# A graph layer on one core: the column sums of the first pass go through VectorE, and a product's first part moves ahead

## What is computed

```python
h   = relu(layernorm(x))                                   # 12500 x 128
m   = concat([h[src], 0, edge_attr]) @ W1 + b1             # 212500 x 256
m   = relu(batchnorm(m, g1, be1))                          # mean and variance over all edges
agg = segment_sum(m, dst) / maximum(count(dst), 1)         # 12500 x 256
n1  = relu(batchnorm(concat([h, 0, agg]) @ W2 + b2, g2, be2))   # 12500 x 385
out = x + relu(n1 @ W3 + b3)                               # 12500 x 128
```

## Time and profile before

| | |
|---|---|
| median of three runs | 3201.42 us |
| the profiled execution, its own time | 3181.97 us |
| its span, first to last instruction | 3180.2 us |
| granted clock of TensorE, mean | 0.856 |
| first pass, first to last gather | 145.9 to 2425.9 us |
| second pass and last stage | 2440 to 3180 us |

### The profile page before, as it was taken

How to read it: one execution, slowest core, us unless ns; L and a number is a source line. 1 busy time by engine, 2 the same in 40 slices (tenths; PEclk the granted TensorE clock), 3 DMA queues, 4 the chain that set the end, 5 groups by cost and what they waited for, 6 DMA issues and landing times. The chain is left out here.

```text
span 3180.2 us, 34295 instructions
## 1 busy us (share of the span) xinstructions
PE 2441.9 (77%) x12138; PEld 914.3 (29%) x12138; DVE 1393.9 (44%) x2299; ACT 969.7 (30%) x1601; POOL 1749.7 (55%) x1850
## 2 busy tenths in 40 slices
PE   4666767657767777777777677777867999999998
PEld 3412112112212222222222122222213433444448
DVE  4422212234323333322333233333223899999878
ACT  3322212112212221222122122212213655655546
POOL 6466666666666666666666666666664222222220
PEclk8888778778878888888888888888876999999999
DMA  8466656666656666666666566566664999999965
GB/s 237 155 210 215 212 194 224 209 221 239 216 194 227 212 213 207 218 204 207 216 229 208 190 223 218 195 228 220 212 206 150 337 350 350 345 343 345 341 238 162
DMA packets 270622, 740.85 MB, mean 233 GB/s; under 512 B 46391, under 2 KB 98661, under 8 KB 270448
## 3 DMA queue, kind: packets, MB, share of 16 engines
q1 hardware_dynamic: 189152, 525.28, 46.2%
q0 software_dynamic: 78432, 212.46, 22.4%
q10 hardware_dynamic: 2864, 0.86, 0.1%
HBM read 501.63 MB, written 236.81 MB: 232 GB/s over the span
## 5 line engine op out<-in xcount | busy, mean ns | idle before, releaser
L621 POOL DMA_INDIRECT sums<-P_d,late x1581 | 1496.5, 947 | 796.4 <-issue 453.3
L1052 DVE TENSOR_TENSOR sums<-psum,sums 128x1024 f32<-128x1024 f32 x396 | 479.0, 1220 | 1524.2 <-remote 823.9
L1351 PE MATMUL psum<-late,sums 128*128 128x512 f32 x1660 | 950.3, 687 | 255.2 <-issue 168.4
L709 ACT ACTIVATE sums<-sums 128x1024 f32<-128x1024 f32 x416 | 437.7, 1054 | 1720.7 <-remote 988.0
L1294 PE MATMUL psum<-sums,ones 128*32 128x512 f32 x830 | 486.5, 667 | 117.8 <-issue 70.2
L1351 PEld LDWEIGHTS psum<-late,sums 128*128 128x128 f32 x1660 | 315.4, 210 | 888.6 <-issue 728.0
L1297 PE MATMUL psum<-sums,ones 128*32 128x512 f32 x830 | 497.9, 676 | 59.5 <-issue 58.6
L1296 PE MATMUL psum<-sums,ones 128*32 128x512 f32 x830 | 494.5, 676 | 36.5 <-issue 35.9
L1295 PE MATMUL psum<-sums,ones 128*32 128x512 f32 x830 | 488.7, 670 | 28.8 <-issue 28.6
L1095 DVE TENSOR_TENSOR late<-late,psum 128x1024 f32<-128x1024 f32 (+1 forms) x407 | 482.6, 1212 | 34.3 <-DMA late<-m_d 32.5
L650 POOL TENSOR_TENSOR late<-dst_f,iota 128x384 f32<-128x384 f32 (+1 forms) x139 | 115.1, 829 | 379.4 <-PE psum L1463 375.3
(11 more groups left out here) (215 smaller groups left out, 2012.0 us busy)
## 6 DMA issues: line engine op xcount, KB each, us to landing
m_d<-sums SPq DMA_DIRECT2D x415, 512.0 KB
late<-m_d SPq DMA_DIRECT2D x406, 512.0 KB, 5.5
sums<-in_ea_main SPq DMA_DIRECT2D x103, 512.0 KB
sums<-P_d,late POOLq DMA_INDIRECT x1581
P_d<-sums SPq DMA_DIRECT2D x24, 512.0 KB
nodes<-in_x SPq DMA_DIRECT2D x24, 256.0 KB
late<-in_x SPq DMA_DIRECT2D x24, 256.0 KB, 3.1
out<-late SPq DMA_DIRECT2D x24, 256.0 KB, 2.4
```

Of the source, the lines that this page charges most:

```text
L621: pool.indirect_dma_start(out=m_s[s][0:r, k * L:(k + 1) * L], out_offset=None, in_=P1_d, in_offset=bass.IndirectOffsetOnAxis(ap=idx[0:r, G ...
L709: act.activation(q_s[g % Q_SLOTS][0:r, 0:w], m_s[g % M_SLOTS][0:r, 0:w], ACT.Square).then_inc(s_q, 1)
L1052: dve.tensor_tensor(m_s[s][0:r, 0:w], ps_m[place_m[g]][0:r, 0:w], m_s[s][0:r, 0:w], ALU.add).then_inc(s_m, 1)
L1351: ins = pe.matmul(ps_m[place_m[g]][:, 2 * i * L:2 * (i + 1) * L], ea[:, i * P:(i + 1) * P], W1c[:, :], start=True, stop=g not in xg_no, sk ...
```

## The change

- The statistics of a full group take two matmuls. ScalarE squares the second half of m into the group's own PSUM buffer, copies the second half of m beside it, and squares the first half into `q_s`. VectorE (`half_sums`) adds the halves of m into `half_s`, and the squares in place, and gives the new semaphore `s_sums`. It does this for group g-1 after the addition of g. PE multiplies `half_s` and `q_s` by the ones.
- What waited for `s_st` to reuse a slot of m (GpSimd's gathers, VectorE's additions in the twenty groups) waits for `s_sums`. ScalarE still waits for `s_st` of g-3, now for the slot that holds squares and half sums.
- A PSUM buffer is free with `s_sums` of its group, no longer with `s_m`.
- `odd_rows(b, 0)` of all 25 blocks moves from the second pass into every second counting step of the first. Its accumulator is now in bank 5 beside the counts, cleared by VectorE at the beginning, and `ps_n` and `empty_bank` use banks 4 and 6 in its place. The weights for k = 0 are ready from the beginning (`s_oddw` counts to 2).
- `totals`, `pick` and the copies at the end of the pass have 64 partitions in place of 128.

```diff
-                act.activation(q_s[g % Q_SLOTS][0:r, 0:w], m_s[g % M_SLOTS][0:r, 0:w], ACT.Square).then_inc(s_q, 1)
+                m, q = m_s[g % M_SLOTS], q_s[g % Q_SLOTS]
+                if g < GF:
+                    act.activation(ps_m[place_m[g]][:, 0:2 * L], m[:, 2 * L:], ACT.Square)
+                    act.activation(ps_m[place_m[g]][:, 2 * L:], m[:, 2 * L:], ACT.Copy)
+                    act.activation(q, m[:, 0:2 * L], ACT.Square).then_inc(s_q, 1)
+                else:
+                    act.activation(q[0:r, 0:L], m[0:r, 0:L], ACT.Square).then_inc(s_q, 1)
...
+            def half_sums(g):
+                m, q, other = m_s[g % M_SLOTS], q_s[g % Q_SLOTS], ps_m[place_m[g]]
+                dve.wait_ge(s_q, g + 1)
+                dve.tensor_tensor(half_s[g % Q_SLOTS], m[:, 0:2 * L], other[:, 2 * L:], ALU.add)
+                dve.tensor_tensor(q, q, other[:, 0:2 * L], ALU.add).then_inc(s_sums, 1)
...
                 if g in ranges:
                     ranges[g]()
+                if g >= 1:
+                    half_sums(g - 1)
...
                 if g >= M_SLOTS:
                     pool.wait_ge(s_mw[s], 16 * (g // M_SLOTS))
-                    pool.wait_ge(s_st, g - M_SLOTS + 1)
+                    pool.wait_ge(s_sums, g - M_SLOTS + 1)
...
-                pe.wait_ge(s_q, g + 1)
-                last = GF - 1
                 if g < GF:
-                    pe.matmul(ps_tot[0:32, :], ones[:, 0:32], m[:, 0:2 * L], ...)
-                    pe.matmul(ps_tot[32:64, :], ones[:, 0:32], m[:, 2 * L:], ...)
-                    pe.matmul(ps_tot[64:96, :], ones[:, 0:32], q[:, 0:2 * L], ...)
-                    ins = pe.matmul(ps_tot[96:128, :], ones[:, 0:32], q[:, 2 * L:], ...)
+                    first, last = g == 0, g == GF - 1
+                    pe.wait_ge(s_sums, g + 1)
+                    pe.matmul(ps_tot[0:SPAN, :], ones[:, 0:SPAN], half_s[g % Q_SLOTS], ...)
+                    ins = pe.matmul(ps_tot[SPAN:2 * SPAN, :], ones[:, 0:SPAN], q, ...)
...
+                if q in own_at:
+                    ins = odd_rows(own_at[q], 0)
                 ins.then_inc(s_cnt, 1)
...
-                    pe.wait_ge(s_xTs if gathered else s_m, i + 1)
+                    pe.wait_ge(s_xTs if gathered else s_sums, i + 1)
...
-                    for b in first_odd_at.get(g, []):
-                        odd_rows(b, 0)
```

More of the change, by code:

```diff
@@ L106, in build @@
     init_at = {early_at[b] if b < EARLY else SG * due[b - 2] + 6: b for b in range(NB)}
-    first_odd = [g for g in range(4, FIRST) if g not in init_at]
-    first_odd_at = {g: [b for b in range(NB) if b * len(first_odd) // NB == i] for i, g in enumerate(first_odd)}
     halves_at = {SG * due[b] - 2 + 3 * h: (b, h) for b in range(NB) for h in range(halves(b))}
@@ L704, in _ @@
             for g in range(NG):
-                r, w = rows(g), tiles(g) * L
+                r = rows(g)
                 act.wait_ge(s_m, g + 1)
@@ L1301, in stats, with odd_rows @@
                 ins.then_inc(s_st, 1)
+            def odd_rows(b, k, start=False):
+                pe.wait_ge(s_oddw, 2 if k else 1)
+                if k:
+                    pe.wait_ge(s_b2, 1)
+                    pe.wait_ge(s_n0, b + 1)
+                v = (nodes, plane[0], plane[1])[k]
+                for t, a, r in tiles_of(b):
+                    ins = pe.matmul(ps_odd[t * SPAN:(t + 1) * SPAN, 0:r], odd_col[:, k, SPAN - 1 - b:2 * SPAN - 1 - b],
+                                    v[:, a:a + r], start=start, stop=(b == NB - 1 and k == KC - 1),
+                                    skip_group_check=True)
+                if k == KC - 1:
+                    ins.then_inc(s_oddacc, 1)
+                return ins
```

62 lines of the change are left out of this document (28 added, 34 removed).

## The result

The changed kernel took 3351.8 us (median of 4 runs, 3342.8 to 3383.6) beside 3202.4 us for the kernel before (3198.4 to 3209.1) on the same chip: a ratio of 1.048, 95% interval 1.041 to 1.056. It is 150 us slower. The forecast was 3149 us, faster; 3352 also lies above the range of 2930 to 3310.

A forecast was written before the change was run, and what follows sets the result against it. GpSimd's gather issue rate was taken as the first pass's floor, with some 330 us of waits on top. Waits -47, own part -7 and pass end +2 made -52 us, from 3201 to 3149 us, range 2930 to 3310.

The forecast's parts named there:

- part 6: PSUM buffers held until s_sums: two-group loop about 4.7 us warm, 6.6 at lower clock, under 2 x 5.0; no steady cost.
- part 4: Slot release for GpSimd's gathers moves two to three groups forward in PE's order: some 10 to 15 us of slack.
- The sum: First-pass wait cycle lengthens from 30.2 to 48 us; 47 waits of 5.2 us, 247 us in place of 294.
- the slow stretches: First-pass times when PE starts few matmuls (11 in 16 us), recurring every 30.2 us with GpSimd waits of mean 3.9 us.
- Part 1: Statistics on PE, four matmuls to two: worth 0 in fast stretches; one and a half times as far in slow ones.
- Parts 2 and 3: ScalarE's three operations take 1.7 us, +0.65 a group; VectorE's two half sums add 1.35 us; both hidden as throughput.
- Part 5: Slot release through VectorE's waiting addition and two half sums: each wait left grows by up to 2.6 us, to 6.5.
- Part 7: Own part of the one-column product leaves the start of the second pass: gain 7 us, bounds 0 and 8.
- Part 8: End of the first pass: last full group goes through three ScalarE operations and half sums, +2 us on the path.
- Rival D: Longer release decides: 75 to 88 waits in the first pass each 1.35 to 2.6 us longer, 3315 us; chance 0.30.
- Rival B: Added slack covers slow stretches that end by themselves, taking nearly all long waits away: about 2900 us; chance 0.18.
- Rival C: Waits come back at the same total at the new gate, net -5 us: 3196 us; chance 0.10.

The follow-up runs named there:

- sbuf_sums: Changed kernel with half sums made from SBUF, one whole-slot ScalarE square, and the PSUM buffer free with the addition again: 3259.0 us, 1.021 of the kernel before.
- hold_only: Kernel before with PE's edge matmuls of group g waiting for VectorE's addition of g-2 in place of g-3, nothing added: 3198.8 us, ratio 1.0035.
- lateness made by hand: Edge matmuls' report given one group later for some 260 of 416 groups: kernel before 3197.4 us, changed kernel 3634.3, half sums from SBUF 3295.6.
- own_only: Kernel before with only the nodes' own part of the one-column product moved behind the counts, no half sums: 3190.6 us, ratio 1.0002.
- the first set: Follow-up runs on one chip with late PE reports, changing buffer hold, half sums, own part or gathers: kernel before 3190.1 us.
- the last set: Kernel before, changed kernel and half sums from SBUF, each with reports delayed, on a chip with late reports: kernel before without the delay 3189.6 us.
- the three between: Second, third and fourth sets of follow-up runs, on chips without late reports: kernel before 2845.3, 2843.9 and 2848.2 us.

## Why the prediction was wrong, point by point

**The failed step is part 6**, the PSUM buffer held until the half sums: "so it costs nothing in a steady state, and eats about 5 us of the slack of part 4". On that the sum took 75 long waits to 47 of 5.2 us. The traces count 74 before and 81 after, 4.0 and 6.0 us each: they didn't get rarer, and each got longer. With the hold undone (sbuf_sums) there are 42, near the 47. So, as far as sbuf_sums tells, the hold ate not 5 us of the slack but all of it.

What part 6 left out of its loop is the time between the end of the edge matmuls and VectorE's knowing of it. As an estimate from the rows: over two groups the loop is 4.7 us + lateness against 2 x 5.0 us, which bears some 5 us of lateness, and here one report in ten is at least 11 to 13 us late. The kernel before frees the buffer with the addition alone, over three groups: 1.92 + 1.22 us + lateness against 15 us, which bears some 12 us. This sum isn't the whole account: by it hold_only (3.1 us + lateness against 10 us) bears some 7 us, less than the latest tenth, and yet it lost only 9 us.

**What is shown and what isn't.** That the loss needs the chips with late reports is shown: 1.048 there, 1.0003 for the same kernel without them. That it goes through the buffer's release by the half sums is shown from two sides: without that release some 80 of 149 us come back, and lateness made by hand adds some 295 us with it, 37 and 8 us without. The 69 us that stay in sbuf_sums stand beside slower gathers (+104 us), which the changed kernel doesn't have; that it would be ahead of the kernel before without them is a sum and not a run, since slower gathers also leave fewer waits. Not shown is how the addition, the two half sums behind it and the rest share the cost: hold_only, the addition alone, cost 9 us, and the runs with ScalarE's square or the column sums in the loop fell on chips without lateness. For the square the trace of the changed kernel speaks: half sums waited 6.3 us in all for it. Open, too, is why PE's reports and its own instructions come late there.

**What bounds the kernel**: the rows were read rightly as to who waits, and only in part as to why. "PE's releases come in bursts" was seen, and the slow stretches were treated as PE running slow, to be shortened by fewer instructions. PE did start instructions late, but the waits end on its reports, and these came late even for matmuls that were long done.

**Part 1**, column sums worth 0 in a fast stretch: right, 0.59 to 0.62 us each pair as before. The bonus for a slow stretch, "one and a half times as far", +8 us of the cycle, has nothing behind it: the long waits came as often as before.

**Parts 2 and 3**: right in size, 1.80 us of ScalarE (0.60 + 0.58 + 0.61, I took 1.7) and 1.36 us of VectorE (1.35).

**Part 4**, slack of two to three groups: sbuf_sums, which has this release and not the hold, has 42 long waits in place of 74, though its slower gathers had a part in that. **Part 5**, each wait longer by up to 2.6 us: by 1.9 us. The sum took half of the 2.6, 1.3.

**Part 7**, own part: I took 7 us. From the first group of the second pass to the end some 5 us went (718.3 and, in own_only, 718.8 us, before 723.6), and own_only as a whole measured 0 (-5 to +6). **Part 8**, +2 us at the end of the pass: 33.3 us in place of 30.7 from the last gather on, one trace each.

**Rival D**, 3315 us with 0.30, is what came, and in its own terms: as many waits as before, each longer by 1.35 to 2.6 us (measured 1.9), and its two signs, waits ended by a half sum and "edge matmuls that wait for s_sums rather than for nothing", are the first rows above. It came out 37 us short; it was priced at its near end, 1.35 us a wait. That reports are late, and that nothing of this happens on other chips, was in no rival. **Rival B** spoke of slow stretches that end by themselves. In the kernel before, 168 of the 209 reports that are over 5 us late come while GpSimd pauses, up to 5.4 us after its last gather ended, and 41 while gathers go on. That fits what the prediction held against B, but as GpSimd waits for these reports, which of the two ends the other isn't shown. **Rival C** is what chips without late reports show, for another reason: in the kernels with these gathers traced there GpSimd has one wait of over 2 us in all.

## What to carry to other kernels

Where a buffer's release passes through an engine's report, put the lateness of the report into the loop beside the operations, and read it from the trace: end of the instruction that raises the semaphore against the start of the one that waited for it. A wait with the releaser "remote" that ends long after the work was done can be such a lateness and not a gap in the record. Count the long waits and their length apart: here their number stayed and their length grew. Measure a change of this kind on more than one chip. Don't let the release of a PSUM buffer go through further work behind its reader in a kernel whose matmul reports are late, even if all the work in the loop is hidden. One group less of room by itself cost 9 us here.

## What the runs showed of the hardware

PE's semaphore increments can be recorded up to 27 us after the matmul that gives them while GpSimd issues indirect gathers all the time (1581 gathers, 1.25 us apart). On the chip of the first set they were at 0.04 us or less without the gathers. VectorE's and ScalarE's recorded increments in the same stretch are at 0.01 us. In the same runs PE stands idle between instructions that nothing holds up (114 us between the column sums of the kernel before, 300 to 2280 us), and a part of the first pass's increments of PE, VectorE and ScalarE is missing from the trace (12 to 41% of a semaphore's in the kernel before). It showed with the result and with the first and the last set, and in none of the three between, with the same kernel: 3190 to 3202 us against 2844 to 2848 us, 12%. What makes a chip one or the other, and whether it stays so, no run tells.

VectorE additions with two operands in SBUF made GpSimd's gathers 1013 ns on average in place of 947, and 1.43 to 1.46 us in the two beside them above; with one operand in PSUM they stay at 948. A plain DMA costs GpSimd 536 ns and, in that kernel, no 0.30 us before it.
